# A fused attention and ternary feed-forward block: the first chunk turned on TensorE with masked keys, weight sums moved to GpSimd

## The reference

```python
x = x + tanh(g_xattn) * attn(layernorm(x), ctx, ctx)     # q,k,v,o: 512x512 with biases, 16 heads
h = relu(s0 * concat(y, -y) @ sign(k0)) * 2              # y = layernorm(x); 1024 -> 2048
h = relu(s1 * h @ sign(k1)) * 2                          # 2048 -> 2048
x = x + tanh(g_ffn) * s2 * h @ sign(k2)                  # 2048 -> 512
```

## Time and profile before

| | us |
|---|---|
| median of 3 runs | 1649.69 (1649.09 to 1650.92) |
| the profiled execution | 1647.89 |
| its span | 1646.1 |
| PE busy | 1518.7 (92%) |
| DVE busy | 953.6 (58%) |
| ACT busy | 679.7 (41%) |
| GpSimd busy | 171.9 (10%) |

### The profile page before, as it was taken

One profiled execution on the slowest core, in us unless ns is written; L12 is line 12 of the kernel. 1 busy time (PEld: TensorE's weight loads), 2 busy tenths in 40 slices (PEclk: granted clock), 3 DMA queues, 4 the chain that ended last, 5 costly groups with the idle time before them and its releaser, 6 DMA issues.

```text
span 1646.1 us, 47594 instructions
## 1 busy us (share of the span) xinstructions
PE 1518.7 (92%) x20152; PEld 1295.8 (79%) x20152; DVE 953.6 (58%) x1947; ACT 679.7 (41%) x1585; POOL 171.9 (10%) x267
## 2 busy tenths in 40 slices
PE   3326789999999999999999999999999999999998
PEld 2214668888888888888888888888888888888887
DVE  2266876565565656565565656566565656566442
ACT  1223425445353534445352534445263534435231
POOL 0031020101101010100101010100101020100100
PEclk7758999999999999999999999999999999999999
DMA  7932232524243332524233342424233342424100
GB/s 217 189 68 64 59 53 59 103 47 98 55 96 67 83 73 59 99 48 101 54 97 65 81 78 59 87 58 98 59 96 61 85 79 59 86 56 101 33 27 15
DMA packets 294714, 126.30 MB, mean 77 GB/s; under 512 B 258408, under 2 KB 275816, under 8 KB 294376
## 3 DMA queue, kind: packets, MB, share of 16 engines
q1 hardware_dynamic: 275880, 114.87, 32.4%
q10 hardware_dynamic: 18624, 8.39, 2.2%
HBM read 38.80 MB, written 17.30 MB: 34 GB/s over the span
## 4 chain that ended last, share of the span: by engine, by line
PE 82%; DVE 8%; ACT 3%; DMA 3%; issue 2%; ACTq 1%; SPq 1%; POOL 0%; DVEq 0%; POOLq 0%
PE bank L1032 22%; PE bank L1033 22%; PE bank L1004 6%; PE bank L1005 6%; PE bank L1046 6%; PE bank L1047 6%; PE bank L981 2%; PE bank L982 2%; PE bank L983 2%; PE bank L957 2%; PE bank L958 2%; PE bank L959 2%; ACTq L272 1%; ACT Pf L532 1%; PE bank L966 1%
## 5 line engine op out<-in xcount | busy, mean ns | idle before, releaser
L1032 PE MATMUL bank<-H,W 128*128 128x128 f16 x7168 | 831.5, 219 | 16.9 <-ACT C L553 14.2
L1033 PE MATMUL bank<-H,W 128*128 128x128 f16 x7168 | 831.6, 219 | 0.0
L1032 PEld LDWEIGHTS bank<-H,W 128*128 128x128 fp8e5 x7168 | 700.1, 98 | 29.6 <-issue 22.1
L1033 PEld LDWEIGHTS bank<-H,W 128*128 128x128 fp8e5 x7168 | 701.7, 98 | 7.5
L1004 PE MATMUL bank<-hT,W 128*128 128x256 f16 x1024 | 229.0, 274 | 10.3 <-DMA hT<-xs 10.3
L1005 PE MATMUL bank<-hT,W 128*128 128x256 f16 x1024 | 228.8, 274 | 0.0
L532 ACT ACTIVATE Pf<-bank,nmax 128x128 f32<-128x128 f32 x512 | 146.0, 368 | 159.1 <-DVE nmax L705 148.9
L436 POOL TENSOR_TENSOR attn<-pvs 128x128 f32<-128x128 f32 x128 | 88.0, 688 | 1096.9 <-DVE pvs L719 1096.9
L1046 PE MATMUL bank<-W,h 128*128 128x512 fp8e5 x512 | 194.0, 379 | 1.6 <-DVE h L751 1.6
L1047 PE MATMUL bank<-W,h 128*128 128x512 fp8e5 x512 | 194.0, 379 | 0.0
L743 DVE TENSOR_TENSOR C<-bank,C 128x256 f32<-128x256 f32 x192 | 81.3, 424 | 168.0 <-ACT C L553 93.3
(11 more groups left out here) (98 smaller groups left out, 1696.5 us busy)
## 6 DMA issues: line engine op xcount, KB each, us to landing
Qst<-q_bounce SPq DMA_DIRECT2D x128, 128.0 KB, 2.8
Y<-in_x_dram SPq DMA_DIRECT2D x16, 512.0 KB, 3.7
q_bounce<-Qhl SPq DMA_DIRECT2D x128, 64.0 KB
R<-X SPq DMA_DIRECT2D x16, 512.0 KB, 3.6
out_dram<-R SPq DMA_DIRECT2D x15, 512.0 KB, 2.6
W<-in_L_ffn_k_dram ACTq DMA_DIRECT2D x8, 512.0 KB, 8.0
PT<-Phl SPq DMA_TRANSPOSE x128, 3.1
H<-in_L_xattn_Wk_dram SPq DMA_DIRECT2D x1, 1024.0 KB, 6.1
```

Of the source, the lines that this page charges most:

```text
L1032: mm(o, w, H0[:, 0, i, b_of, :], start=first, stop=False, skip_group_check=True)
L1033: last = mm(o, w, H0[:, 1, i, b_of, :], start=False, stop=i == PAIRS - 1, skip_group_check=True)
```

## The change

- The attention of chunk 0 turns everything on PE: matmuls with the identity into PSUM (`turn_four`), with ACT taking the high part from PSUM and DVE the low part. No transposing DMA stands in its path.
- The queries and keys of chunk 0 don't go through memory. The keys of a group are copied four times side by side, each copy masked to the rows of one head (`Kb`, `own_head`), so that four matmuls of 128x512 give the scores of a unit. The masked copies (KM) and the low part of the keys are made on GpSimd. The bounce of the keys remains, for chunk 1 on.
- Units of attention start after the first group of keys and queries, and the others are made between them. DVE adds the halves of the attention output of chunk 0 itself.
- All large loads go to SP in order of use, before anything that waits; ACT issues only the small ones, at the start. The last two loads of k1 and the bounce of the keys stand behind the values' projections in SP's list.
- The front of chunk 1 (LN, N1, T1) goes ahead of the output projection of chunk 0 on every engine.
- W0 is made on GpSimd (four sums of 128x2048 fp8, after two shifts on DVE), and three of the four sums of each group of W1 too. DVE keeps the signs and S1. All of W1 and W2 is now made during chunk 0.

```diff
+    FIRST = [(0, (kind, n)) for kind, n in (
+        ("CX", 0), ("CX", 1), ("LN", 0), ("LN", 1), ("N1", 0), ("N1", 1), ("K", 0), ("T1", 0), ("T1", 1), ("KM", 0),
+        ("SCALARS", 0), ("CUT_Q", 0), ("CUT_Q", 1), ("CUT_Q", 2), ("CUT_Q", 3), ("XB", 0), ("XB", 1),
+        ("Q", 0), ("K", 1), ("KM", 1))]
+    BETWEEN = {0: [("Q", 1)], 1: [("V", 0)], 2: [("K", 2), ("KM", 2), ("CUT_O", 0)], 3: [("Q", 2), ("CUT_O", 1)],
+               4: [("K", 3), ("KM", 3), ("CUT_O", 2)], 5: [("Q", 3), ("CUT_O", 3)], 6: [("V", 1), ("K0", 0), ("W0", 0)],
+               7: [("W0", 1)], 8: [("W0", 2)]}
+    for k in range(U + 2):
+        FIRST += [(0, ("S", k))] if k < U else []
+        FIRST += [(0, item) for item in BETWEEN.get(k, ())]
+        FIRST += [(0, (kind, k - behind)) for kind, behind in (("PT", 1), ("PV", 2)) if 0 <= k - behind < U]
+    FIRST += [(0, ("CT", 0)), (0, ("CT", 1))]
+    FIRST += [(1, (kind, t)) for kind in ("LN", "N1", "T1") for t in range(TT)]
+    FIRST += [(0, item) for item in (("WO", 0), ("WO", 1), ("N2", 0), ("T2", 0), ("N2", 1), ("T2", 1), ("W0", 3))]
+    LATE_SIGNS = {1: 0, 8: 1, 14: 2, 20: 3}
+    LATE_SUM = {4: 0, 11: 1, 17: 2, 23: 3}
+    LATE_SUMS = {1: (0, 0), 3: (0, 1), 5: (0, 2), 8: (1, 0), 10: (1, 1), 12: (1, 2),
+                 14: (2, 0), 16: (2, 1), 18: (2, 2), 20: (3, 0), 22: (3, 1), 24: (3, 2)}
...
+            sp.wait_ge(n1_ready, NT)
+            sp.wait_ge(xb_ready, NT)
+            load(Y_flat, x_v[1], x_loaded)
+            load_k1(sp, 0)
+            load(W2[:, :, :].bitcast(u32), by_rows(k2), k2_in)
+            load_k1(sp, 1)
+            sp.wait_ge(v_done, BATCHES)
+            load_k1(sp, 2)
+            sp.wait_ge(wq_lo, KT)
+            load_k1(sp, 3)
+            sp.wait_ge(k_lo, KT)
+            for a in range(2):
+                sp.dma_start(k_dram[a].rearrange("d m j n -> j d m n"), KHL[:, a, :, :]).then_inc(k_kept, 16)
...
+                if kind == "W0":
+                    if n == 0:
+                        pool.wait_ge(k0_shifted, 2)
+                    pool.tensor_tensor(W0[:, n, :], W0[:, n, :], k0_b[:, n, :].bitcast(f8), ALU.subtract,
+                                       saturate=False)\
+                        .then_inc(w0_made, 1)
+            def weight_sum(q, n):
+                Wg = W1[:, q]
+                L11, L12, L21, L22 = (Wg[:, b] for b in range(4))
+                if n == 0:
+                    pool.wait_ge(w1_signs, q + 1)
+                    pool.tensor_tensor(Wg[:, A_S3], L11, L21, ALU.subtract, saturate=False).then_inc(w1_sums, 1)
+                if n == 1:
+                    pool.wait_ge(w1_sums, 3 * q + 1)
+                    pool.tensor_tensor(Wg[:, A_S2], L22, Wg[:, A_S3], ALU.subtract, saturate=False)\
+                        .then_inc(w1_sums, 1)
+                if n == 2:
+                    pool.wait_ge(w1_sums, 3 * q + 2)
+                    pool.wait_ge(w1_sum, q + 1)
+                    pool.tensor_tensor(Wg[:, A_S4], L12, Wg[:, A_S2], ALU.subtract, saturate=False)\
+                        .then_inc(w1_sums, 1)
...
+                    if once and n == 0:
+                        act.wait_ge(k_kept, 32)
+                        act.wait_ge(v_lo, BATCHES)
...
+                if kind == "S":
+                    g, t = divmod(n, TT)
+                    pe.wait_ge(q_lo, g + 1)
+                    pe.wait_ge(k_masked, 2 * g + 2)
+                    for i, (hl_q, hl_k) in enumerate(((0, 0), (1, 0), (0, 1), (1, 1))):
+                        last = mm(bank[:, :], Qhl[:, g % 2, hl_q, t * P:(t + 1) * P], Kb[:, hl_k, g, :],
+                                  start=i == 0, stop=i == 3)
```

More of the change, by code:

```diff
@@ L281, in _ @@
             load(ctx_f, ctx.rearrange("(b p) d -> p b d", p=P), ctx_in)
+            load(Y_flat, x_v[0], x_loaded)
             load(Wk_f, by_rows(Wk), wk_in)
[L283 to L287, removed]
@@ L312, in attend @@
                     k = CUT[kind] + n
[L313 to L314 removed]
+                    wait_apart(sp, xs_lo, nth(a - 1, NX, k))
+                    if kind == "T1":
                         wait_apart(sp, wo_done, nth(a - 1, NT, NT - 1))
@@ L317, in attend @@
                         wait_apart(sp, q_done, nth(a, NG, NG - 1))
-                    if kind == "T2" and not first:
+                    if kind == "T2":
                         wait_apart(sp, l0_done, nth(a - 1, NP, NP - 1))
@@ L384, in _ @@
[L384 to L391, removed]
+            for f in range(CHUNKS - 1):
+                for s, slot in enumerate(SLOTS):
+                    for ahead, item in woven(s, f == CHUNKS - 2):
+                        attend(item, f + ahead)
+                    if f and slot == ("L2P", GROUPS - 1, 1):
+                        store(f - 1)
+                    if f and slot == ("L1", 0, P6):
+                        sp.wait_ge(out_stored, nth(f - 1, 16, 15))
+                        keep_x1(f)
@@ L493, in prepare, with exponents @@
                     nc.scalar.activation(c[:, 0:2], scal[:, 0:2], ACT.Tanh).then_inc(const_tanh, 1)
-                if item == ("T2", 0):
-                    act.wait_ge(const_step, 3)
-            def attend(item, a, first=False):
-                kind, n = item
-                bank = banks[(FIRST_BANK if first else LOOP_BANK)[item]] if kind in ON_PE else None
+            def exponents(n, a, bank):
+                act.wait_ge(s_max, nth(a, NU, n))
+                if a or n >= 2:
+                    act.wait_ge(p_lo, nth(a, NU, n - 2))
+                for j in range(4):
+                    last = nc.scalar.activation(
+                        Pf[:, n % 2, j * P:(j + 1) * P], bank[:, j * P:(j + 1) * P], ACT.Exp,
+                        bias=nmax[:, n % 2, j:j + 1], scale=1.0)
+                last.then_inc(p_ready, 1)
@@ L523, in attend @@
[L523 to L535 removed]
+                    query_parts(n, a, bank)
@@ new lines, in _ @@
+            for f in range(CHUNKS):
+                for s, slot in enumerate(SLOTS):
+                    kind, q, h = slot
+                    feed(slot, f, f == 0)
+                    if kind == "L2":
+                        second_feed(q, h, f, f == 0)
+                    if kind == "L2P" and f:
+                        second_feed(q, h, f - 1)
+                    if f < CHUNKS - 1:
+                        for ahead, item in woven(s, f == CHUNKS - 2):
+                            attend(item, f + ahead)
```

762 lines of the change are left out of this document (386 added, 376 removed).

## The result

The changed kernel takes 1626.38 us (median of 4 runs, 1625.3 to 1626.61) against 1649.49 for the kernel before (4 runs, 1649.09 to 1650.92): ratio 0.9857, 95% interval 0.984 to 0.9874. It is 23 us faster; the forecast was 1640, 9.6 us faster, with a range of 1606 to 1664.

The account below looks back on a forecast made before the run. Latency was taken to bound the prologue and DVE chunk 0: L0 at 103 us, chunk 0 of 145 and 1388.5 unchanged make 1636.5 of span, 1638.3 profiled, 1640.1 as median (9.6 us faster); range 1606 to 1664.

Parts of the forecast that it names:

- What bounds the kernel, and 1388.5 us behind: Whole kernel: latency bounds the prologue, DVE bounds chunk 0, PE the rest; 1388.5 us after chunk 0 stay the same.
- The front: Start of the prologue: the first maximum of an attention unit comes at 29 us in place of 66.20.
- The units: Prologue's attention rounds of chunk 0: eight at 5.2 us, 4 more for V 1's round, about 4 for W0 sums.
- The tail: Prologue from whole attention (79 us) to L0, layer one's start: 24 us, so L0 at 103, 34.3 earlier.
- The keys' bounce: Prologue, SP's list: lands near 90 us, 13 us ahead of ACT's first work of L0, which waits for it.
- Holds: Prologue and chunk 0: a GpSimd sum holds DVE's operations with two SBUF inputs for its whole length.
- the first rival: Chunk 0: GpSimd's fp8 sums don't hold DVE, chunk 0 takes about 100 us and the kernel 1589; chance 0.12.
- The price of a sum: GpSimd in prologue and chunk 0: 4.5 us for a 128x2048 fp8 sum; twelve in chunk 0 make 54 us.
- The allowance of 9 us: Chunk 0: 9 us added for PE's lowered clock and engine-to-engine latency, within the forecast 145 us.
- The second rival: Prologue and chunk 0: fp8 sums on GpSimd take longer than f32; at 6 us each the time is 1662; chance 0.22.
- The third: Rival, prologue: PE's clock stays at half through the attention rounds; eight cost 18 us, time 1658; chance 0.10.
- The sum: Whole kernel: prologue -34.3 us plus chunk 0 +24.7 makes -9.6 us, 0.6% faster.

Follow-up runs that it names:

- writes_only: The changed kernel with each of GpSimd's twelve W1 sums in chunk 0 replaced by two memsets of the same block (output not the reference's): 1596.35 us, ratio 0.9666.
- before_gpsimd_sums: The kernel before, with S3, S2 and S4 of W1's groups 1 to 3 moved from DVE to GpSimd in their old slots: 1658.74 us, ratio 1.0051.
- fp8_price: The changed kernel with eighteen trial sums on GpSimd in its last chunk, six sizes and types (f32, f16, fp8) three times each: 1626.14 us in one run.
- group3_gpsimd: The changed kernel with W1's sums on DVE, placed in its gaps and spread over chunk 0, but group 3's three sums on GpSimd: 1608.44 us, ratio 0.9745.

## Why the prediction was right or wrong, point by point

- **What bounds the kernel, and 1388.5 us behind.** Right: 1388.4.
- **The front.** 31.8 us for 29. Right within 3.
- **The units.** 5.2 us a plain round, as taken. The rounds with the last key projection and with V 1 were longer: 50.73 to 58.17 is 7.4, and the round with V 1 is 14.0 (63.38 to 77.37), where I had 5.2 + 4. Of its 14.0, 2.6 are the hold of a W0 sum (2.87 for 0.29), which I had counted apart; the two such holds together cost 4.9 us for the 4 that I gave them. DVE waits 4.97 us for V 1. Its eight f32 matmuls took 5.81 us on PE at a granted clock of 0.65, against 3.60 for the same eight of V 0 at 1.00:

```profile
33.80 3.60 PE L1007 MATMUL bank<-W,hT 128*128 128x512 f32 x8
...
63.20 5.81 PE L1007 MATMUL bank<-W,hT 128*128 128x512 f32 x8
```

  The eight of a key projection took 3.62 us at 0.54 in the long round, against 1.89 at 1.00 in the one of 5.4 (from 40.10). Attention was whole at 86.0 for 79: of the 7 us, 3 are the front, about 4 the clock in these two rounds, and 1 the holds, less 1 elsewhere.
- **The tail.** 19.2 us for 24. The front of chunk 1 took 5.2 us as forecast. The turned attention output (CT) took 2.5 for 4.5, the two sums with statistics 3.4 for 4.5, and the norm with W0's last sum and the turn 8.1 for 8.5; my terms add up to 22.75, where I wrote about 23 to 25 and took 24. The hold of the second norm that I had counted is there (L814, 2.52 us in place of 0.54), shorter because DVE came to it 1.6 us after the sum had begun (99.81 and 98.22). So **L0 at 105.2 for 103, 32.1 earlier for 34.3**: right, with two errors of 5 to 7 us against each other, which is luck.
- **The keys' bounce.** It issues at 75.58 and lands before L0; nothing waited for it, as I had it.
- **Holds.** The mechanism is right, shown by `writes_only`, `before_gpsimd_sums` and the rows above; the first rival (fp8 sums don't hold, 1589) is refuted. With the holds of the twelve sums taken away the kernel takes 1596, 7 us over that rival's time; W0's are still in it.
- **The price of a sum: the first mis-sized term.** 4.5 us, measured 3.82 to 3.94 in ten of the twelve (5.81 and 4.15 in the others, where DVE was at work too). 12 x 0.65 = 7.8 us of the 14.1 by which chunk 0 was taken too long (145 for 130.9). I drew the line through the 1.26 us of an f32 sum of two different tensors; with the slope of fp8, 1.78 ns, it would have given 3.87 (`fp8_price`). With 3.85 the list to slot 25 gives 101 - 7.8 = 93.2, and DVE was done with slot 25 at 95.4 us into the chunk (200.6 on the trace).
- **The allowance of 9 us: the second.** From there to the end of chunk 0 it takes 236.1 - 200.6 = 35.5 us, with PE busy for all 35.50 and a clock of 1.00. The last low part of slot 25, and the stretch behind it:

```profile
198.65 1.94 DVE L831 SCALAR_TENSOR_TENSOR h<-C,h 128x256 f16<-128x256 f32 x1 [1.18 <-ACT h L667]
```

```profile
200.60:236.10 35.50, 35.50 (x485) 28.89 (x483) 18.23 (x39) 8.21 (x19) 6.76 (x11) 1.00 0.37 68
```

  So I had 9 us for the clock and for latency where the trace has about half a microsecond: ahead of slot 25 the clock is 0.82 (105.2 to 200.6), but that is hidden where DVE is the bound, as I had said myself, and behind it nothing is lost. The list with its 101 for 95.4 gives 5.6 of the 14.1 (7.8 for the price, less 2.2 by which it was otherwise longer), and this stretch with 44 for 35.5 the other 8.5.
- **The second rival, slower by dearer fp8** (1662): refuted by `fp8_price`. **The third, the clock at half in the rounds** (1658): granted is 0.85 from 31.8 to 63.4 and 0.77 over the prologue, against 0.67 before. A low clock (0.54 and 0.65) lengthened two rounds, not the eight. Whether the turns count for the clock no run shows.
- **The sum.** -32.1 + 10.6 = -21.5 us of span for -9.6. The sign and the mechanism are as forecast, the gain more than twice the forecast one. The step that failed is the length of chunk 0, 145 us for a measured 130.9: the price of a sum (4.5 for 3.85 us) and the allowance of 9 us for clock and latency (0.5) were both too high. The prologue's 2.2 us the other way hid a part of it. The time lies in the range, which is wide: 58 us for a difference of 23.
- **What I did not see** is that the same work had a better place. In a round DVE waits for ACT behind the maximum; the trace of before has that too (the low part begins 1.73 us after DVE is free), and I read it as latency only, not as room for a sum.

## What to carry to other kernels

Before a two-input operation is moved from DVE to GpSimd, write down what DVE does meanwhile. If it is SBUF work, the move can cost GpSimd's duration (3.85 us) instead of DVE's (2.29), and here nine such moves made the kernel 8 us slower. First look for gaps of the busy engine about as long as the operation, such as a wait behind a reduction that another engine must answer: six operations in such gaps added 10.7 us of DVE work to the prologue and left the start of L0 within 0.5 us. And extrapolate a duration only from rows of the same type and kind of operands, and add no allowance to a stretch that a later stretch of the same trace shows undisturbed.

## What was unexpected of the hardware

The holds were forecast, with their length (some 4 us) and the hold of a norm among them. The runs add:

- A hold lasts to the end of GpSimd's operation however short the held one, in fp8 as in f32: 0.29 us became 3.80.
- It takes in a DVE operation with one f32 tensor input and two scalars (0.54 became 4.04, `group3_gpsimd`).
- Mere writes of GpSimd leave DVE's two-input operations alone, but two u32 operations on weights took 1.71 and 2.23 us beside memsets in `writes_only`, in place of 1.28. My theory of reads doesn't cover these.
- A sum of GpSimd in fp8 costs 1.78 ns an element from 512 to 2048 elements, and f16 costs 1.93 (first pass); the f32 sum of two different tensors (1.26 us at 512) lies above the trial sums of 512 in all three types (1.04 to 1.16). The reason for that row stays open.
